# Two attention phases and two routed feed-forwards: the gate cut into two runs, drain and fill steps put between feed-forward steps, the set-up block dissolved

## What is computed

```python
x = x + attention_a(layernorm(x))   # 16 heads of 8, biases, two masked scores per head
x = x + ffn(layernorm(x))           # top 2 of 8 experts per item
x = x + attention_b(layernorm(x))
x = x + ffn(layernorm(x))

def ffn(x):
    pooled = x.mean(axis=1)                        # one row per item
    gate = softmax(pooled @ gate_w.T)
    top_w, top_i = top_k(gate, 2); top_w /= top_w.sum() + 1e-08
    h = gelu(x @ down_w[top_i].T + down_b[top_i])  # 2 x 64 hidden
    return sum_k(top_w[k] * (h[k] @ up_w[top_i[k]].T + up_b[top_i[k]]))
```

## Time and profile before

| | us |
|---|---|
| median of 3 runs (lowest, highest) | 1039.98 (1037.24, 1041.08) |
| the profiled execution's own time | 1038.88 |
| its span | 1037.0 |
| TensorE busy, share of the span | 913.8, 88% |
| DVE | 788.4, 76% |
| ACT | 759.8, 73% |
| POOL | 595.9, 57% |
| mean granted clock of TensorE | 0.965 |
| transferred | 131.64 MB, mean 127 GB/s |

### The profile page before, as it was taken

One profiled execution on the slowest core, in us unless ns is written; L12 is line 12 of the kernel. 1 busy time (PEld: TensorE's weight loads), 2 busy tenths in 40 slices (PEclk: granted clock), 3 DMA queues, 4 the chain that ended last, 5 costly groups with the idle time before them and its releaser, 6 DMA issues. The chain is left out here.

```text
span 1037.0 us, 27550 instructions
## 1 busy us (share of the span) xinstructions
PE 913.8 (88%) x10204; PEld 519.3 (50%) x10204; DVE 788.4 (76%) x1398; ACT 759.8 (73%) x1324; POOL 595.9 (57%) x1011
## 2 busy tenths in 40 slices
PE   2379999999999999984876999999999999998577
PEld 1235555555555555442753455555555555554266
DVE  0388888888888888843448899899999999885244
ACT  1147888888888888783752888888888888888466
POOL 4555666666666666422355566666666666643211
PEclk9989999999999999997897999999999999999779
DMA  8545555455554544300035554544555545540023
GB/s 238 169 148 145 147 144 145 144 150 142 145 152 145 144 142 151 107 3 21 2 104 157 151 154 140 151 150 149 143 151 151 147 146 144 156 129 3 1 59 106
DMA packets 140516, 131.64 MB, mean 127 GB/s; under 512 B 9880, under 2 KB 121888, under 8 KB 140256
## 3 DMA queue, kind: packets, MB, share of 16 engines
q1 hardware_dynamic: 139312, 128.49, 42.6%
q10 hardware_dynamic: 1072, 1.40, 0.5%
HBM read 73.75 MB, written 55.57 MB: 125 GB/s over the span
## 5 line engine op out<-in xcount | busy, mean ns | idle before, releaser
L379 DVE TENSOR_REDUCE nmax<-ring 128x4 f32<-128x1024 f32 x512 | 607.8, 1217 | 74.1 <-PE ring L504 73.8
L418 ACT ACTIVATE probs<-ring 128x1024 f32<-128x1024 f32 x512 | 510.3, 1027 | 49.7 <-PE ring L521 46.4
L486 PE MATMUL values_bank<-probs,values 128*32 128x256 f32 x4096 | 274.1, 385 | 5.9 <-ACT probs L418 5.9
L504 PE MATMUL ring<-k_stack,q_stack 64*128 64x256 bf16 x2048 | 201.7, 278 | 42.9 <-DMA k_stack<-scratch 23.1
L335 POOL TENSOR_SCALAR xy<-x,mv,rstd 128x128 f32<-128x128 f32 x256 | 202.1, 800 | 8.7
L521 PE MATMUL ring<-q_stack,k_stack 64*128 64x256 bf16 x2048 | 187.4, 273 | 0.7 <-DVE nmax L379 0.4
L486 PEld LDWEIGHTS values_bank<-probs,values 128*32 128x32 f32 x4096 | 106.8, 109 | 90.4 <-issue 23.4
L298 POOL TENSOR_SCALAR mparts<-nmax 128x32 bf16<-128x32 f32 x64 | 13.9, 218 | 230.2 <-DVE nmax L379 230.2
L504 PEld LDWEIGHTS ring<-k_stack,q_stack 64*128 64x128 bf16 x2048 | 74.6, 95 | 139.0 <-ACT probs L418 67.3
L521 PEld LDWEIGHTS ring<-q_stack,k_stack 64*128 64x128 bf16 x2048 | 83.9, 95 | 75.4 <-issue 36.9
L450 ACT COPY values<-m_bank 128x128 f32<-128x128 f32 x128 | 29.0, 278 | 81.6 <-PE m_bank L565 81.6
(11 more groups left out here) (99 smaller groups left out, 1028.9 us busy)
## 6 DMA issues: line engine op xcount, KB each, us to landing
q_stack<-scratch SPq DMA_DIRECT2D x128, 256.0 KB
k_stack<-scratch SPq DMA_DIRECT2D x128, 256.0 KB
scratch<-parts SPq DMA_DIRECT2D x128, 192.0 KB, 2.5
scratch<-parts SPq DMA_DIRECT2D x128, 128.0 KB, 2.5
scratch<-parts SPq DMA_DIRECT2D x128, 64.0 KB, 3.1
out<-x SPq DMA_DIRECT2D x32, 128.0 KB, 1.8
q_stack<-maxT SPq DMA_DIRECT2D x128, 12.0 KB
scratch<-in_tail SPq DMA_DIRECT2D x8, 128.0 KB, 3.3
```

The lines of the kernel that those rows point to most:

```text
L379: nc.vector.tensor_reduce(dst, src, axis=AX.X, op=ALU.max, negate=True).then_inc(max_done, 1)
L418: nc.scalar.activation(probs[g % 2][:, c:c + 2, :, :], pair_of_exps(n, p)[:, :, :].rearrange("p x (k q) -> p x k q", k=TILES), ACT.Exp).th ...
L486: last = nc.tensor.matmul(values_bank[32 * c:32 * (c + 1), a * TOKENS:(a + 1) * TOKENS], values[item % RING][:, k, PER_GROUP * g + c, :], ...
L504: last = nc.tensor.matmul(pair_of_scores(n, p)[:, a, t * TOKENS:(t + 1) * TOKENS], q_stack[z][rows, p, t * P:(t + 1) * P], k_stack[z][rows ...
```

## The change

Four things are changed together.

1. The set-up block is gone. Its parts open the first attention block (`opening`), without a barrier behind them. ACT waits for three early loads (wa, ident, wb) before it scales; TensorE waits for the scaled weights; the other users of constants, memsets and scratch rows wait where they first need them. POOL sets three more small tensors (`wide`, `hot`, `mix`).
2. x comes in six chunks: two at the opening, the others issued by SP at the end of attention a's steps -1 to 2.
3. The gate is in pieces and runs twice per feed-forward (`gates`): for items 0 to 27 in attention's step 31, one piece behind a pair each, and for all 32 between feed-forward steps 9 to 14. Tensors that both runs write and the feed-forward reads are doubled. The pieces use `m_bank`.
4. `run` ends at step 31 and, for b, begins at -1. The drain steps 32 to 34 are put between feed-forward steps -2 to 7 (`BEFORE`), and b's steps -6 to -2 between steps 8 to 32 of the first feed-forward (`AFTER`), in pieces of one to eight pairs; for that a step's program emits one pair per call. POOL's splitting is cut into four pairs' pieces. The feed-forward's PSUM moves to one of the three `ring` tensors, half of a second, and the bank of the values; b's step -2 then uses one `ring` tensor for its scores and all other filling steps use two.

```diff
-CONSTANTS = 11
-CHUNKS = ((0, 2), (2, 9), (9, ITEMS))
+EARLY_LOADS, CONSTANTS = 3, 8
+CHUNKS = ((0, 2), (2, 9), (9, 15), (15, 21), (21, 27), (27, ITEMS))
...
+        def scalar_opening(act):
+            early = [(wa[:, :], attn_w[:, :]), (ident[:, :], ident_c[:, :]), (wb[:, :], attn_b[:, :])]
...
+            act.wait_ge(early_in, 16 * EARLY_LOADS)
+            nc.scalar.copy(identb[:, :], ident[:, :])
+            nc.scalar.mul(bqs[:, :], wa[:, 512:513], float(HEAD) ** -0.5)
+            nc.scalar.mul(wa[:, 0:WIDTH], wa[:, 0:WIDTH], float(HEAD) ** -0.5)
+            nc.scalar.mul(wb[:, 0:WIDTH], wb[:, 0:WIDTH], float(WIDTH) ** -0.5).then_inc(weights_ready, 1)
+            act.wait_ge(weights_ready, 1)
...
+        def tensor_opening(pe):
+            pe.wait_ge(weights_ready, 1)
...
-                return ring[2 * (n * PAIRS + p) % 3]
+                i = n * PAIRS + p
+                return ring[2 * i % 3 if i >= 0 else i % 2 if i >= SINGLE else 0]
...
+            SINGLE = -2 * PAIRS if masked else -PAIRS
...
+                    if n == -3:
+                        sp.wait_ge(tail_in, 4 * 16 if masked else 2 * 4 * 16)
...
+                    if masked and 2 <= n + 3 < len(CHUNKS):
+                        load_x(sp, n + 3)
...
+            def tensor_logits(pe):
+                fill_m(pe, dve_g, 1)
+                pe.wait_ge(yT_ready, rows)
+                pe.wait_ge(consts_in, 16 * CONSTANTS)
+                nc.tensor.matmul(m_bank[of_run, 0:EXPERTS], pooled[:, of_run], gate_sb[:, :], start=True, stop=True).then_inc(pe_g, 1)
+
+            def tensor_transposes(pe):
+                fill_m(pe, dve_g, HOT_T)
+                pe.wait_ge(dve_g, MIXED)
...
+            programs = {"tensor": {1: tensor_logits, 5: tensor_transposes, 7: tensor_biases}, "scalar": {3: scalar_exps},
+                        "vector": {2: vector_best, 4: vector_top, 6: vector_weights, 8: vector_biases},
+                        "sync": {4: sync_index}, "gpsimd": {}}
...
+        EARLY = ITEMS - RING
...
+                for n in range(first, ITEMS):
+                    for p in range(PAIRS):
+                        phase["slot"](step, n, p)
+                        piece = gate["programs"][kind].get(p + 1)
+                        if n == ITEMS - 1 and piece:
+                            piece(engine)
...
+            BEFORE = {-2: (32, 0, 3), 0: (32, 3, 4), 1: (32, 4, 7), 2: (32, 7, 8), 4: (33, 0, 8), 7: (34, 0, 8)}
+            GATE = {9: (1, 2), 10: (2, 3), 11: (3, 4), 12: (4, 5), 13: (5, 7), 14: (7, 9)}
+            AFTER = {8: (-6, 0, 8), 10: (-5, 0, 3), 14: (-5, 3, 8), 15: (-4, 0, 3), 16: (-4, 3, 6), 17: (-4, 6, 8),
+                     18: (-3, 0, 3), 19: (-3, 3, 6), 20: (-3, 6, 8), 21: (-2, 0, 1), 23: (-2, 1, 2), 25: (-2, 2, 3),
+                     27: (-2, 3, 6), 30: (-2, 6, 7), 32: (-2, 7, 8)}
+            down_bank = [ring[2][:, i, 0:TOKENS] for i in range(2)]
+            up_bank = [values_bank[:, 0:TOKENS], ring[1][:, 0, 0:TOKENS]]
...
+                for n in range(-AHEAD, ITEMS + BACK):
+                    if n in BEFORE:
+                        of_step, first, end = BEFORE[n]
+                        for p in range(first, end):
+                            before["slot"](old, of_step, p)
+                    for turn in range(*GATE.get(n, (0, 0))):
+                        if turn in gate_of[1]["programs"][kind]:
+                            gate_of[1]["programs"][kind][turn](engine)
+                    if after and n in AFTER:
+                        of_step, first, end = AFTER[n]
+                        for p in range(first, end):
+                            after["slot"](new, of_step, p)
                     emit(n, n % RING, lambda k: 0 <= n + k < ITEMS)
...
-                    nc.scalar.preload_act_table(ACT.Gelu)
...
+        run(phase_a, -6, gate_a[0], opening)
+        feed_forward("fa", phase_a, gate_a, phase_b, False, x_given[0])
+        run(phase_b, -1, gate_b[0])
+        feed_forward("fb", phase_b, gate_b, None, True, x_given[1])
```

## The result

| | before | after |
|---|---|---|
| median of the timed runs | 1039.07 us | 1041.87 us |
| profiled execution: span | 1037.0 us | 1044.0 us |
| mean granted TensorE clock | 0.965 | 0.953 |

The ratio of the changed kernel to the one before, run beside each other, is 1.0034, 95% interval 1.0023 to 1.0045. So the change is 3.5 us slower, which is under the half per cent that the prediction counted as measurable, where 27 us of gain had been forecast. The profiled execution took 1045.8 us, at the slow end of the timed ones (1037.1 to 1045.8), so the spans differ by more than the medians. The next table cuts both profiled spans at the same events. "Forecast" is what the prediction's terms give for each, moved to these events (the prediction counted a feed-forward to DVE's last sum, 0.4 to 0.5 us more).

What follows compares the result with a forecast made beforehand. TensorE, 97% busy, fills the steady stretches; gains lie elsewhere: opening 8.9, a to b 10.4, end 8.1, so 27.4 off 1038.9 gives 1011.5, and 1.1 for the median makes 1012.5 us. Range for 8 in 10: 996 to 1028.

Steps and rivals of the forecast that it cites:

- Steady stretches: Long middle stretches of both attentions: same instructions in the same order per engine, so nothing gained.
- Opening: Kernel start without the barrier: first transposes at 9.1 us instead of 18.52; 8.9 us gained after 0.5 for a chunk.
- First gate run in step 31: End of each attention: step 31 takes 3.5 us longer with the gate's pieces in TensorE's line, bounds 0 and 8.
- Second gate run: Each feed-forward: 6.0 us added, as 2.6 tables, 0.3 and 3.1 waits half covered by two items' lead; bounds 3 and 8.
- The clock: TensorE after the drain-and-gate stretches: 0.5 us won back per feed-forward, granted clock 1.00 through the gates.
- Drain: Last attention steps, 12.7 us alone, moved into each feed-forward: 3.8 us added there, bounds 2.3 and 12.7.
- Fill of b: b's steps in a's feed-forward: -6 to -3 cost 6 instead of 8.2, -2 costs 7; 11.9 follow instead of 22.0.
- The base: Each feed-forward without added pieces: 8 fours of items at 5.13 us, 41.0 us.
- Lockstep: Rival: pieces add in full as TensorE stands at m_bank; feed-forwards 80 and 62, total 1046 us, chance 0.04.
- 999: Rival of nearly full overlap: stretches bound by engine sums, not waits; feed-forwards 57 and 48, gain 39.6 us, chance 0.19.
- 1024: Rival of much lost to waits: feed-forwards 70 and 56 us, gain 15 with the opening, chance 0.17.
- the table switches of the second gate run: ACT in each feed-forward: two more table loads of 1.28 us, 2.6 us per feed-forward.

Runs made afterwards that it cites:

- e1: Changed kernel with all undone but the opening and the chunks of x (feed-forward loop stays unrolled); 1030.4 us, ratio 0.9923 to the kernel before.
- e3: e1 plus the changed kernel's two gate runs, drain and fill of b still as before the change; 1047.2 us, ratio 1.0086 to the kernel before.
- e5: e4 with the first gate run's pieces moved within step 31 (exponential two slots earlier, transposes one later); 1030.7 us, ratio 0.9917 to the kernel before.
- e7: e4 with the identity in place of the second gate run's exponential, so no table loads there; 1037.4 us, ratio 0.9971 to the kernel before.
- e8: e4 with six unused matmuls ahead of the second gate run's transposes on TensorE; 1032.6 us, ratio 0.9925 to the kernel before.
- e4: Changed kernel with only the fill of b undone, so e3 with the drain in the feed-forward; 1037.3 us, ratio 0.9987 to the kernel before.
- e10: e1 plus b's steps -6 to -2 in the feed-forward, -6 to -3 earlier than in the change, -2 in single slots; 1026.2 us, ratio 0.9881 to kernel before.
- e11: Changed kernel, both gate runs' pieces re-placed, b's fill at items 8 to 32, Gelu table first, second exponential a POOL power; 1015.2 us, 0.9769 to kernel before.
- e12: e11 with the second gate run's last pieces later, at items 18 and 20, behind b's steps -6 to -3; 1014.4 us, ratio 0.9743 to the kernel before.

## Why the prediction was wrong, point by point

**In short.** The step that failed is the price of the pieces put in line on TensorE. The prediction sized them by the engines' free time and waits half covered, and took the clock as a small gain. The runs show each gate run at 5.4 to 9.6 us where 3.5 and 6.0 were said, and the fill of b as a loss of 4.3 to 4.6 us where a gain of 5.3 was said, because TensorE stands for the last of what a piece waits for, and part of the work behind runs at half clock.

**Steady stretches: right.** From 76 to 441 us TensorE is busy 355.35 us, as before, and b's attention is longer by 5.9 us, 5.6 of them its step 31.

**Opening: right.** The transposes came at 8.55 where 9.1 was said (8.6 as the near bound), and the part alone gave 8.5 us (e1) where 8.9 was said.

**First gate run in step 31: the term was mis-sized.** 3.5 us were said per phase, with 8 as the far bound; the runs show 6.1 and 5.4 (e3 less e1). The 2.71 us for DVE's chain is what had been counted. Not counted were the second wait at m_bank (1.35) and the clock: from 460.00 to the end of step 31 it is 0.50. e5 took 3.3 and 2.7 us away up to the last exponentials by placing the pieces alone, and 1 us more each ahead of the first down matmul. The other half of the term, what leaves the stretch ahead of the feed-forward, was 8.1 in the sum and 5.4 and 6.1 on the chip.

**Second gate run: mis-sized, and for a wrong reason.** 6.0 us per feed-forward were said, 2.6 of it tables; 9.6 and 8.5 were measured (e3 less e1). The tables are 1.0 to 1.1 of that in items 8 to 16 (e7). The prediction let two items of lead cover half of a wait of up to 3.4 us. In the trace TensorE stood 3.79 us in full, and then three items ran at half clock; e8 gives 2.4 us of a's items 8 to 16 back, and 2.8 of b's, without shortening DVE's chain.

**The clock: taken with the wrong sign.** The prediction took it as a gain (0.5 us back, granted clock 1.00 through the gates), because the two long idle stretches would be gone. They were cut into many waits, and the clock was low in stretches behind them: 0.50 at the end of step 31, 0.79 over a's feed-forward, where the earlier trace rows had 0.94. In the second gate runs alone keeping the clock up gave 4.7 to 6.4 us (e8). The rows of a half-clock start were there to be read (3.13 us for the first three items' down matmuls, 11.2 us for the first eight items), and it was priced once, not once per wait.

**Drain: right in the sum, by luck in part.** Its terms give 5.1 us per phase, and e3 to e4 shows 5.0. But 8.9 us were to leave the stretch ahead of the feed-forward (12.7 less the 3.8 of the start), and 11.8 and 10.4 did; 3.8 were to come back inside, and 5.7 and 5.9 did. The two misses cancel. The first of them is the other side of the 2 to 2.7 us by which the removal of the gate fell short: both parts share that stretch.

**Fill of b: wrong.** 5.3 us of gain were said, 4.3 and 4.6 of loss were measured. Step -2 was costed by DVE's eight reductions; what came on top was the transfer ahead of it, 6.5 and 7.0 us. The prediction had the number, "about 9.4" us for such a load (in the trace 9.3), and a 3.41 us wait for one. It used them for the chunks of x and for item 2, not for item 0, whose loads the schedule puts three items ahead of their use. With room for them, and step -2 in single slots, the part gave 4.2 (e10).

**The base: wrong in the sum.** 8 x 5.13 was taken for the whole stretch. From first to last down matmul b takes 41.0 us before the change and 41.2 in e1, but the last item's up matmuls end 2.6 later. That tail is missing in b, and in a it was booked on b's steps. The gain for the clock, 0.5 in each feed-forward and 0.9 more in a, was not there either.

**Sum of the misses.** The gates cost 16.8 us where 2.8 were said, which is 14.0; the fill cost 4.6 where 5.3 of gain were said, which is 9.9; the base holds what is left of the forecast's 27.4 us of gain, 5.8. With the opening and the drain as said this is the 30 us between 1012.5 and 1042.

**The rivals.** "Lockstep" (a's feed-forward 80, b's 62, 1046 in all, chance 0.04) came nearest: 82.4, 58.3 and 1041.9. Its mechanism, that TensorE stands at m_bank for another engine in each piece, is in part what the traces show: those waits are there, for DVE and ACT, but the largest single one is a transfer, which it doesn't name. Its near sum in a is luck in part: it had 13 us for the drain, where 5.7 came, and 10 for step -2, where the fill of b adds 17.2 (82.4 against 65.2 in e4). The argument against it, that a normalising step left two fours at their pace, took a piece without a long wait for all of them. The prediction called itself wrong if a's feed-forward passed 72, and it did. Two prices of rivals, 999 and 1024, leave out the 1.1 us between the profiled execution and the median that the forecast has; with it they are 1000 and 1025.

With the pieces placed otherwise, about the forecast time was reached: e11 and e12, 1015 and 1014. They leave out the table switches of the second gate run, for which the forecast had 5 us, so they don't show that its terms were right. They show that a time near it can be had, and that the order given in the change did not reach it.

## What to carry to other kernels

When a piece of work is put in line on an engine that runs its instructions in order, cost it by the latest of what it waits for, a transfer's landing first. Then count how much work stands between the issue of what it needs and its use. Busy sums only say what a perfect order could reach. Where TensorE idles, look at the granted clock behind the wait, and price the wait with it. Put each part of a change in alone: here two parts were gains and two were losses, and placing the losing two otherwise turned a loss of 3.5 us into a gain of 24.

## What the hardware showed that was not expected

**Work without use can pay.** In e8 six matmuls in each feed-forward that nobody reads made the kernel 4.7 us faster by the medians and 6.4 by the ratios; TensorE was granted 1.00 behind them instead of 0.50.

**A DVE instruction is held up under some of POOL's operations.** In the changed kernel's timelines of DVE and POOL:

```profile
513.91 1.21 DVE L859 TENSOR_SCALAR wu<-up_sb,weight 64x128 f32 x1
```

```profile
513.88 1.16 POOL L369 TENSOR_TENSOR rest<-qk,parts 128x512 f32<-128x512 f32 x1
```

The same DVE instruction took 284 ns in the mean in a's feed-forward before, and 416 after, over 32 of them. The long ones begin while POOL splits q and k (128x512) and end within 0.1 us of its instruction's end. DVE's sums from PSUM (414 ns in the mean, 417 before) kept their time. The Trainium skill, "SBUF — State Buffer", section "Who interferes with whom", says that DVE in its two-port modes and GpSimd take one shared pair of ports by an exclusive lock, and that the second to start is blocked to the end of the first; these rows agree, though no row shows in which mode DVE ran. Other rows do not: beside POOL's normalising (L356, 128x128, 0.80 us) the same DVE instruction, begun inside it at 472.68 and 535.50, took 0.30 and 0.28 us and ended before it. Why it is held up under the one and not under the other stays open. In all it cost 4.2 us of DVE time. No run tested what that did to the kernel's time, so it is no part of the explanation above.

**A table load costs its own row.** The next activation begins 1.29 us after the load does (475.48 and 476.77), and 1.30 after each of the two of the second gate run (498.39 and 499.69, 500.09 and 501.39). The Trainium skill's 1380 ns of drain on top ("ScalarE: Activation LUTs", "What ACT_TABLE_LOAD costs") is in none of these rows. Leaving four loads out gave neither 5.1 us, four of their rows, nor 10.6 (e7, 1.7 by the ratios).
